# Token sums moved into the second expert stage, the mixing's differences onto TensorE and its normalisations onto ScalarE

## The reference

```python
x = x + tanh(g_xattn[0]) * attention(layernorm(x), ctx_2048)        # heads within a token
x = x + tanh(g_ffn[0])   * experts_0(layernorm(x))                  # 16 experts, top 6, and a shared one
x = x + tanh(g_xattn[1]) * wkv(layernorm(x), ctx_2048)              # 64 sequences of 64 steps
x = x + tanh(g_ffn[1])   * experts_1(layernorm(x))                  # 64 experts, top 8
```

```python
no = maximum(o, u + k);  A = exp(o - no);      E = exp(u + k - no)
y  = (A * p + E * v) / (A * q + E)
no2 = maximum(w + o, k); A2 = exp(w + o - no2); E2 = exp(k - no2)
p, q, o = A2 * p + E2 * v, A2 * q + E2, no2
```

```python
final = sum over e of combine[:, e] * ((silu(x @ gate_e) * (x @ up_e)) @ down_e)
```

## Time and profile before

| | us |
|---|---|
| median of 3 runs | 2355.81 |
| profiled execution | 2351.87 |
| its span | 2350.1 |
| stage M, from its barrier to the next (1229.2 to 1754.5) | 525 |
| stage H1 (1754.5 to 2240.4) | 486 |
| stage I1 (2240.4 to 2350.1) | 110 |

### The profile page before, as it was taken

One profiled execution on the slowest core, in us unless ns is written; L12 is line 12 of the kernel. 1 busy time (PEld: TensorE's weight loads), 2 busy tenths in 40 slices (PEclk: granted clock), 3 DMA queues, 4 the chain that ended last, 5 costly groups with the idle time before them and its releaser, 6 DMA issues. The chain is left out here.

```text
span 2350.1 us, 35817 instructions
## 1 busy us (share of the span) xinstructions
PE 1636.8 (70%) x9250; PEld 1208.8 (51%) x9250; DVE 1325.7 (56%) x3592; ACT 682.7 (29%) x1894; POOL 1045.3 (44%) x1039
## 2 busy tenths in 40 slices
PE   2959976888439999999964344441109999999800
PEld 1437754555227777777742222221108888888700
DVE  5113325656315555555536999999705555555557
ACT  1422221222013333333322222222005555555400
POOL 4031003677733333333330166666656666666600
PEclk9979986988769999999987666665559999999955
DMA  4595646533435757666314244544766666666489
GB/s 142 182 147 69 97 63 245 186 120 114 160 112 183 264 195 245 211 229 225 114 60 171 89 158 159 177 148 160 260 260 184 190 187 194 191 190 192 147 336 378
DMA packets 237104, 419.22 MB, mean 178 GB/s; under 512 B 90496, under 2 KB 170496, under 8 KB 231424
## 3 DMA queue, kind: packets, MB, share of 16 engines
q1 hardware_dynamic: 164080, 215.58, 32.3%
q0 software_dynamic: 48144, 138.57, 16.1%
q10 hardware_dynamic: 24704, 62.98, 7.7%
HBM read 253.36 MB, written 209.88 MB: 197 GB/s over the span
## 5 line engine op out<-in xcount | busy, mean ns | idle before, releaser
L896 PE MATMUL ps<-w_all,h_xT 128*128 x2112 | 546.1, 381 | 5.2 <-ACT h_xT L1119 5.2
L913 PE MATMUL ps<-w_all,h_hT 89*128 (+1 forms) x1472 | 409.7, 383 | 2.5
L640 POOL DMA_INDIRECT y_b<-h_y,h_ix x320 | 310.1, 969 | 174.9 <-issue 127.9
L623 POOL DMA_INDIRECT xs_b<-h_x,slot_of x256 | 270.9, 1058 | 244.0 <-DVE slot_of L1474 168.2
L896 PEld LDWEIGHTS ps<-w_all,h_xT 128*128 128x128 f32 x2112 | 343.3, 191 | 53.3 <-issue 9.2
L640 POOL DMA_INDIRECT y_a<-h_y,h_ix x208 | 201.7, 970 | 350.0 <-DVE h_y L1638 341.1
L889 PE MATMUL ps<-ident,h_x 128*128 128x128 f32 x1056 | 203.8, 274 | 115.3 <-DMA h_x<-xs_a 61.2
L1638 DVE TENSOR_SCALAR h_y<-ps,h_sum 128x256 f32<-128x256 f32 x528 | 254.6, 482 | 38.6 <-issue 22.8
L913 PEld LDWEIGHTS ps<-w_all,h_hT 89*128 89x128 f32 (+1 forms) x1472 | 239.2, 191 | 29.8 <-issue 6.5
L1119 ACT COPY h_xT<-ps 128x256 f32<-128x256 f32 x528 | 196.1, 371 | 151.9 <-PE ps L889 136.0
L623 POOL DMA_INDIRECT xs_a<-h_x,slot_of x192 | 190.0, 990 | 105.9 <-issue 57.9
(11 more groups left out here) (232 smaller groups left out, 2129.4 us busy)
## 6 DMA issues: line engine op xcount, KB each, us to landing
xs_b<-void_d ACTq DMA_DIRECT2D x40, 1128.0 KB, 13.1
h_x<-xs_b SPq DMA_DIRECT2D x80, 564.0 KB
c_a<-y_b SPq DMA_DIRECT2D x8, 4096.0 KB, 13.1
h_x<-xs_a SPq DMA_DIRECT2D x52, 564.0 KB, 4.2
k_a<-y_a SPq DMA_DIRECT2D x16, 1536.0 KB, 8.2
w_all<-in_exp SPq DMA_DIRECT2D x7, 2560.0 KB
qkv_d<-a_out ACTq DMA_DIRECT2D x8, 1536.0 KB, 7.4
w_all<-in_exp SPq DMA_DIRECT2D x4, 2432.0 KB
```

Of the source, the lines that this page charges most:

```text
L623: pool.indirect_dma_start(xs_d[L.name], bass.IndirectOffsetOnAxis(ap=slot_of[:, g * GT + j, k:k + 1], axis=0), h_x[:, g % NB, j, :], None) ...
L640: pool.indirect_dma_start(y_d[L.name], bass.IndirectOffsetOnAxis(ap=h_ix[:, s:s + 1], axis=0), h_y[:, s % YB, :], None).then_inc(q["y_st"] ...
L896: m = pe.matmul(ps[:, 2 + s % 2, 0:2 * L.H], h_xT[:, s % 2, c, :], w_all[:, bass.ds(e * L.W + c * 2 * L.H, 2 * L.H)], start=(c == 0), stop ...
L913: m = pe.matmul(ps[:, 6 + s % 2, 0:D], h_hT[0:w, s % 2, j, :], w_all[0:w, bass.ds(e * L.W + L.up0 + j * D, D)], start=(j == 0), stop=(j == ...
```

## The change

There are three parts.

**Differences (M).** `exponents` keeps the scan and `w_max`. The four differences become pairs of products on TensorE, one with the identity and one with its negative (`minus`), into PSUM banks 5 to 7 in turn, and ScalarE takes the exponential of each from PSUM, w and u being added as its bias. Other PSUM banks and both engines' orders change with it.

**Normalisations (M).** VectorE computes rstd and -mean*rstd for the four tiles of a group, and ScalarE writes the normalised rows, with them as scale and bias.

**Token sums (H1, I1).** 28 of the 32 token tiles are summed within H1, each at a fixed step: a token tile's 8 results are loaded as two halves of 512 KB, one into what was the fourth slot of `h_x` (NB_OF is 3 for this layer), and x from `x_d` (128 KB). VectorE's adds are spread over four steps behind the tile's own work. The four tiles of the last group are left for I1.

```diff
+SUM_ROOM = 8
+NB_OF = {"a": NB, "b": NB - 1}
+        def tiles_of_groups(n):
+            return NTOK // NG * L1.K // P * n + L1.E - 1
+        sum_at = {}
+        for t in range(NT - GT):
+            ready = tiles_of_groups(t // GT + 1) + SUM_ROOM
+            sum_at[t] = ready + (8 if t // GT < NG - 2 else 6) * (t % GT)
+        halves = [h_x[:, NB - 1].rearrange("p j c -> p (j c)")[:, 0:CHOICES // 2 * D], s_b[:]]
 # SP, stage H1: token_in(t) is called behind batch (sum_at[t] - SUM_ROOM + 3) // HB + nb - 1
+            def token_in(t):
+                if t % GT == 0:
+                    n = tiles_of_groups(t // GT + 1)
+                    for s in range(YB):
+                        sp.wait_ge(lay["b"]["y_st"][s], 16 * ((n - s + YB - 1) // YB))
+                if t:
+                    sp.wait_ge(s_done, t)
+                of = of_tokens(L1)[t // GT, :, t % GT, :]
+                for h in range(2):
+                    sp.dma_start(halves[h], of[:, h * CHOICES // 2 * D:(h + 1) * CHOICES // 2 * D]).then_inc(s_in[h], 16)
+                if t >= 2:
+                    sp.wait_ge(out_st, 16 * (t - 1))
+                sp.dma_start(s_x[:, t % 2], x_d[:, t * D:(t + 1) * D]).then_inc(sx_in, 16)
+                if t:
+                    token_out(t - 1)
 # VectorE, stage H1: part p of token tile t in step sum_at[t] + p
+                def add_token(t, part):
+                    if part < 2:
+                        a = halves[part]
+                        dve.wait_ge(s_in[part], 16 * t + 16)
+                        dve.tensor_tensor(a[:, 0:2 * D], a[:, 0:2 * D], a[:, 2 * D:4 * D], ALU.add)
+                    elif part == 2:
+                        dve.drain()
+                        dve.tensor_tensor(halves[0][:, 0:2 * D], halves[0][:, 0:2 * D], halves[1][:, 0:2 * D], ALU.add)
+                        dve.drain()
+                        dve.tensor_tensor(halves[0][:, 0:D], halves[0][:, 0:D], halves[0][:, D:2 * D], ALU.add)
+                    else:
+                        dve.wait_ge(sx_in, 16 * t + 16)
+                        dve.drain()
+                        dve.scalar_tensor_tensor(x_t, halves[0][:, 0:D], gate, x_t, ALU.mult, ALU.add)\
+                           .then_inc(s_done, 1)
 # TensorE, stage M
+            def differences(g, c):
+                o_prev, o_now = w_o[:, c, :, 0:SEQ], w_o[:, c, :, 1:SEQ + 1]
+                key, largest = w_k[:, c, :, 1:SEQ + 1], w_max[:, c]
+                pe.wait_ge(wk_t, 2 * g + c + 1)
+                for v, (a, b) in enumerate(((o_prev, o_now), (key, o_now), (o_prev, largest), (key, largest))):
+                    n = 4 * (2 * g + c) + v
+                    if n >= 3:
+                        pe.wait_ge(wk_exp, n - 2)
+                    pe.matmul(ps[:, spread[n % 3], :], ident[:], a, start=True, stop=False)
+                    pe.matmul(ps[:, spread[n % 3], :], minus[:], b, start=False, stop=True).then_inc(wk_less, 1)
 # TensorE's order in stage M
                 if g:
                     states_back(g - 1)
+                if g < NG:
+                    differences(g, 0)
+                    differences(g, 1)
+                if g:
+                    turned(L1, g - 1)
+                    logits(L1, g - 1, e_g1)
                 if g + 1 < NG:
                     choices_summed(g + 1)
                 if g:
-                    turned(L1, g - 1)
-                    logits(L1, g - 1, e_g1)
                     ranks(L1, g - 1)
 # ScalarE: decays(g, 0), decays(g, 1), deviations(g-1), rows_normalised(g-1), turned, exponentials_of(g-1),
 #          key_deviations(g+1), keys_normalised(g+1), keys_turned(g+1)
+            def scaled(g, dst):
+                for j in range(GT):
+                    t = g * GT + j
+                    m = act.activation(dst[:, j, 0:D], x_res[:, t, :], ACT.Identity, bias=mean[:, t:t + 1],
+                                       scale=rstd[:, t:t + 1])
 # VectorE, stage M
-                dve.tensor_tensor(w_t[:, c, 0], o_prev, o_now, ALU.subtract)
-                dve.tensor_tensor(w_t[:, c, 1], key, o_now, ALU.subtract)
-                dve.tensor_tensor(w_t[:, c, 2], o_prev, w_max[:], ALU.subtract)
-                dve.scalar_tensor_tensor(w_t[:, c, 3], key, u, w_max[:], ALU.add, ALU.subtract).then_inc(wk_t, 1)
+            def scale_of(part):
+                dve.reciprocal(rstd[:, part], rstd[:, part])
+                dve.drain()
+                return dve.scalar_tensor_tensor(mean[:, part], mean[:, part], -1.0, rstd[:, part], ALU.mult, ALU.mult)
```

More of the change, by code:

```diff
@@ L236, in flamingo @@
             s_ = sb_in(st)
[L237 removed]
+            s_("h_x", [P, NB, HB, RW])
+            c_a = s_("c_a", [P, GT, CHOICES * D])
+            c_x = s_("c_x", [P, GT, D])
             assert nc.sbuf_base <= nc.sbuf_top - big
@@ L470, in slots, with token_out @@
+            def token_out(t):
+                sp.dma_start(out_v[t], s_x[:, t % 2]).then_inc(out_st, 16)
             def slots(L):
                 q = lay[L.name]
+                nb = NB_OF[L.name]
                 rows = xs_d[L.name].rearrange("(n p) c -> p n c", p=P)
[L475 to L479, removed]
+                load_at = {}
+                if L is L1:
+                    for t, step in sum_at.items():
+                        load_at.setdefault((step - SUM_ROOM + 3) // HB + nb - 1, []).append(t)
@@ L480, in slots @@
                 n = L.tiles // HB
[L482 to L509, removed]
+                for m in range(max(n, max(load_at, default=0) + 1)):
+                    if m < n:
+                        if m >= nb:
+                            sp.wait_ge(q["t_done"], HB * (m - nb + 1) + 2)
+                            sp.wait_ge(q["ix_ready"], m - nb + 1)
+                        sp.dma_start(h_x[:, m % nb], rows[:, m * HB:(m + 1) * HB, :]).then_inc(q["x_in"][m % nb], 16)
+                    for t in load_at.get(m, []):
+                        token_in(t)
@@ L555, in _ @@
             end_stage(sp, "H1")
[L557 to L560, removed]
-                sp.dma_start(o_v[bass.ds(g, 1)].rearrange("a p t d -> (a p) t d"),
-                             x_res[:, bass.ds(g * GT, GT), :]).then_inc(out_st, 16)
-            sp.wait_ge(out_st, 16 * NG)
+            sp.wait_ge(s_done, NT - GT)
+            token_out(NT - GT - 1)
+            for j in range(GT):
+                t = NT - GT + j
+                sp.dma_start(c_x[:, j], x_d[:, t * D:(t + 1) * D]).then_inc(c_in[j], 16)
+                sp.dma_start(c_a[:, j], of_tokens(L1)[NG - 1, :, j, :]).then_inc(c_in[j], 16)
+            for j in range(GT):
+                sp.wait_ge(c_done, j + 1)
+                sp.dma_start(out_v[NT - GT + j], c_x[:, j]).then_inc(out_st, 16)
+            sp.wait_ge(out_st, 16 * NT)
             end_stage(sp, "I1")
@@ L1655, in body @@
                         if s % HB == 0:
-                            compare(j, s // HB, b)
+                            compare(j)
                         elif s % HB == 1:
-                            pick(s // HB)
+                            pick(j)
                         elif s % HB == 2:
                             place_of(s // HB)
+                        if L is L1:
+                            for t, part in adds_at.get(j, []):
+                                add_token(t, part)
                 dve.memset(h_oh[:], 1.0)
@@ L1817, in _ @@
                     chosen_experts(L1, g - 1)
-                if g < NG:
-                    over_time(g, 1)
+                if g + 1 < NG:
+                    keys(g + 1)
                 if g:
                     slots_of(L1, g - 1)
-                if g + 1 < NG:
-                    keys(g + 1)
                 if g < NG:
@@ L1829, in _ @@
             end_stage(dve, "H1")
-            sums(L1, tgate[:, 3:4])
+            for j in range(GT):
+                dve.wait_ge(c_in[j], 32)
+                dve.tensor_tensor(c_a[:, j, 0:4 * D], c_a[:, j, 0:4 * D], c_a[:, j, 4 * D:8 * D], ALU.add)
+                dve.drain()
+                dve.tensor_tensor(c_a[:, j, 0:2 * D], c_a[:, j, 0:2 * D], c_a[:, j, 2 * D:4 * D], ALU.add)
+                dve.drain()
+                dve.tensor_tensor(c_a[:, j, 0:D], c_a[:, j, 0:D], c_a[:, j, D:2 * D], ALU.add)
+                dve.drain()
+                dve.scalar_tensor_tensor(c_x[:, j], c_a[:, j, 0:D], tgate[:, 3:4], c_x[:, j], ALU.mult, ALU.add)\
+                   .then_inc(c_done, 1)
             end_stage(dve, "I1")
```

168 lines of the change are left out of this document (88 added, 80 removed).

## The result

Before: a median of 2356.34 us in five runs (2355.72 to 2361.91). After: **2370.03 us** in five runs (2368.74 to 2371.54). The change makes the kernel slower by 0.4 to 0.9%, 13 to 17 us, where "no change" was forecast.

What follows compares the result with a forecast made beforehand. DMA was taken to bound I1, TensorE H1 and VectorE M; 2351.9 - 89.5 (I1) + 64 (M) + 24 (H1) = 2350.4 us profiled, which lay 3.9 below the median, so forecast 2355 us, range 2326 to 2394.

Steps and rivals of the forecast that it cites:

- I1, -89.5: Stage I1: with four token tiles left it falls from 109.7 to 20 us, bounds -92 and -86.
- M, period 64.0: Stage M: the hand-over chain lengthens a group from 54.14 to 64.0 us, +9.8, +59 over six iterations.
- M, the first iteration, +4.7: Stage M: without routing, it still waits for TensorE's products; keys chain ends after some 41 us against 36.3.
- H1, 0.61 a token tile: Stage H1: TensorE waits 0.61 us per token tile for VectorE's longer adds, 17 us over 28 tiles.
- the slack of 0.45: Stage H1: `hidden` ends 0.45 us before TensorE needs it, subtracted from VectorE's lateness of 0.74 + 0.32.
- H1, late loads, 4 + 3: Stage H1: group 6's three token loads late by about 1.3 us each, 4 us; 3 us for the rest.
- The signs of being wrong: M's period under 60; H1 waits on the halves' DMAs above 10 us in all; TensorE waiting for h_x.
- the rival of late loads: Stage H1: token loads come late on nearly full DMA, 1.3 us more per tile, 36 us, 2391 us; chance 0.30.
- Stages before M, 0: Stages A to H0: no change in time, forecast 0.
- the high clock through M: Stage M: TensorE keeps its high clock, 3.6 us less a group, 22 us, 2333; chance 0.20 shared with sums fitting H1.
- the sums did not fit in H1: Stage H1: rival that slack absorbs the sums, H1 only +8, 2339 us; chance 0.20 shared with the high clock.
- its 7.9 a group: Stage M: rival that all VectorE work removed is gained, 7.9 us a group, 55 in all, 2235 us; chance 0.05.

Runs made afterwards that it cites:

- e12: Changed kernel with choices' products summed one iteration earlier in two PSUM banks of their own: 2300.5 us (before 2355.3), ratio 0.9769.
- e13: As e12, with VectorE's and ScalarE's order rewritten, rows' scales ahead of both halves of over_time: 2267.1 us (before 2355.3), ratio 0.9635.
- e10: Kernel of before with only the normalisations of rows and keys moved to ScalarE: 2366.7 us (before 2354.5), ratio 1.0049.
- e9: The changed kernel run again, unaltered: 2371.8 us (before 2354.5), ratio 1.0070.
- e14: As e11, with each token sum cut into five parts for four: 2300.0 us (before 2355.3), ratio 0.9759.
- e2: Mixing alone: stage M of the changed kernel, H1 and I1 as before, on a slower chip: 2729.6 us (before 2620.5), ratio 1.0439.
- e3: Same kernel as e12 on a slower chip: 2620.6 us (before 2620.5), ratio 0.9991.
- e11: Token sums alone: H1 and I1 of the changed kernel, stage M as before: 2300.0 us (before 2355.3), ratio 0.9762.
- e1: Same kernel as e11 (token sums alone) on a slower chip: 2528.8 us (before 2620.5), ratio 0.9666.
- e4: Same kernel as e13 on a slower chip: 2579.5 us (before 2620.5), ratio 0.9870.

## Why the prediction was wrong

The sum was right in its mechanism and off in the size of two terms: -1.5 us forecast and +16.7 measured. The step that failed is the price of the two losses: M was put at +64 and measured +71.2, H1 at +24 and measured +32.4. In M the period of 64.0 was too short by about 1, in H1 the 0.61 a token tile should have been 0.80, and 3 us of late loads and group ends were missing; 0.8 more came in I1 and 1.8 ahead of M. The sum lay within 5 us of no change between terms of 89 and 88, so a term that was off by a tenth was enough to make a clear loss of it. The time still lies inside the range of 2326 to 2394, which was wide enough to hold a gain as well as a loss.

- **I1, -89.5.** Measured -88.7: right. (20 us were expected, 21.0 came.)
- **M, period 64.0.** Measured 66.2, 65.1, 64.7, 64.9, 65.1, 64.8 for the six iterations with the whole chain: 390.8 for 384, **+6.8**. The steps from T, forecast and measured (T = 1434.63 in the rows above): last exponential 17.6, 18.1; scale ready 19.6, 20.1; rows normalised 21.6, 22.2; transposes 23.6, 24.2; logits 28.4, 29.1; choices' products 39.9, 40.9. Every step was in its place, in its order and at the clock that I took; the delay was 0.5 at the last exponential (the first two products of differences took 2.08 and 1.29 us for 1.02 each behind them) and grew to 1.0 (the choices' products took 12.04 for 11.5). What is behind choices_added took 23.8 for 24.1. The first of the six is the longest: there the first three products took 2.08, 1.91 and 1.23, and the choices' products 12.53. The square root began 1.29 us after its table load (1452.79 to 1454.08), so no more than the load itself stands on the path.
- **M, the first iteration, +4.7.** Measured 42.0 for 36.3, +5.7. With the periods this makes 7.8, and the start and the end of M take back 0.6 of the 7.2 us by which M was missed. e12 and e13 show that the mechanism was the right one; e10 that the normalisations, which I booked as a gain on VectorE with their delay on the chain, are by themselves, in this order, a loss of 9 us of M.
- **H1, 0.61 a token tile.** Measured 0.80 where the loads are in time: 28 x 0.19 = **5.3 us** short. `hidden` is late by 0.76 behind part 2 (2.18 - 1.416; 0.74 forecast) and by another 0.40 behind part 3 (1.82 - 1.416; 0.32 forecast, without the gap of 0.16 before L1728), 1.17 in all for 1.06. Less the slack of 0.45 that is 0.72; the 0.08 left to 0.80 are not broken down.
- **H1, late loads, 4 + 3.** Of 32.4 us, 28 x 0.80 = 22.4 are the regular price; 10.0 are left for the first tokens of groups, group 6, and late loads, for 7 forecast. Group 6 was nearly right: the last 24 tiles took 41.6 us for 34.8 (by GpSimd's stores), of which 2.4 are the regular price of three token tiles, so 4.4 for 4; in e9, the same kernel, it was 5.7. One term rested on the wrong rows: the landing in 4.2 us of the earlier trace rows is that of H0's loads, since the trace of before has no landing for a load of H1. After the change the first halves landed in 4.5 to 5.1 us; no landing of a second half is in the trace.
- **The signs of being wrong.** The period of M was not under 60. VectorE's waits for the halves' loads made 7.9 us, under the 10 that I had named (8.9 in e9). TensorE did wait for h_x, twice and 2.4 us in all, where it did not before. So the rival of late loads was right in kind and small; e14 shows how near it is: one step later and the waits for the halves are 19.9 us.
- **Stages before M, 0.** Measured +1.8. GpSimd's last store of the first experts' results began at 1218.3 us before and between 1219.4 and 1223.1 in the seven other profiles at this pace, the changed kernel's two at 1220.0 and 1219.9; e14 with the old M has the largest. What makes this spread of 5 us stays open.

The rivals: the high clock through M did not come (the transposes took 1.97 after 4.86 us without work, the logits 3.68), and the sums did not fit in H1, which would have cost 8 there. M did not gain its 7.9 a group: VectorE got 7.1 us less work and the group became 10.6 longer.

## What to carry to other kernels

Work moved off the engine that bounds a loop pays only if the new path is shorter than that engine's remaining work: here 7 us a group were taken from VectorE and the period grew by 11; putting the choices' products, which now stood behind the routing in TensorE's order, elsewhere took 13 off it again. When an engine gets new work, write out again where its old work should stand, and give it room an iteration ahead (here two PSUM banks). And where a forecast is a small difference of large terms, its sign rests on tenths of a microsecond that repeat in every group and tile. The chances said so, with 0.42 for slower and 0.38 for faster; the single figure of 2355 us did not.

## What the runs showed that I had not expected

**The same kernel at two paces.** H1 without any sums took 485.0 us before and 594.7 in e2, from the same instructions. In M the two kinds of chips differ most in ScalarE's exponentials. Three of its rows in e3, while GpSimd scatters, then the same three in e12, the same kernel at the first pace:

```profile
1702.47 0.60 ACT L1255 ACTIVATE w_e<-ps 128x512 f32<-128x512 f32 x1 [5.67 <-issue]
1713.00 0.60 ACT L1255 ACTIVATE w_ex<-ps 128x512 f32<-128x512 f32 x1 [9.93 <-remote]
1723.50 0.69 ACT L1257 ACTIVATE w_ex<-ps,w_wu 128x512 f32<-128x512 f32 x1 [9.90 <-remote]
```
```profile
1422.29 0.60 ACT L1255 ACTIVATE w_e<-ps 128x512 f32<-128x512 f32 x1 [1.03 <-PE ps L985]
1424.01 0.60 ACT L1255 ACTIVATE w_ex<-ps 128x512 f32<-128x512 f32 x1 [1.12 <-PE ps L985]
1425.72 0.69 ACT L1257 ACTIVATE w_ex<-ps,w_wu 128x512 f32<-128x512 f32 x1 [1.12 <-PE ps L985]
```

The operands of the first three were there: by its timeline TensorE's products for them ended at 1696.7, 1698.4 and 1700.1. GpSimd's last scatter of that group began at 1720.11, and the long gaps end with it; in e12 the scatters run at the same rate, one in 1.27 us, and the gaps are 1.1. The three gaps make 25.5 us, and that group took 75.2 us for 51.3 in e12. In H1 the gaps are short and many: in 200 us of e2 ScalarE waited 26 us in 53 pieces for nothing that the profile shows on this core, the longest 3.2, and in 200 us of H1 before not at all. H0, where the scattered stores are 2.5 us apart, took the same 524 us on both kinds of chips. So the loss goes with dense scattered stores; that they cause it, and why only on some chips, no run tells. What it means for a design does show: the version with eight hand-overs between TensorE and ScalarE in each group beside scatters lost 4.4% there (e2) for some 3% here (72 of 2300 us), so e13's gain is 3.7% on one kind of chip and 1.3% on the other, while the sums alone gain 2.4% and 3.4%.

**A sign that turns with the chip.** e13 is the fastest kernel at 2355 us for before (2267 against 2300 for e11), and e1 the faster one at 2620 (2529 against 2579 for e4). A comparison of two versions on one chip would have picked either.
